# Self-attention's weights turned on VectorE in squares of 32, summed by row tiles of 32 keys, and projected by eight masked products

## What is computed

```python
x = x + self_attention(layernorm(x))        # causal, with a relative-position bias
x = x + cross_attention(layernorm(x), ctx)  # 77 context tokens
x = x + experts(layernorm(x))               # 8 routed experts, top 2, and a shared one
```

```python
q, k, v = split_heads(x @ Wq + bq), split_heads(x @ Wk + bk), split_heads(x @ Wv + bv)
logits = where(j <= i, (q @ k.T + bias(q @ rel_key.T)) * scale, -inf)
attn = softmax(logits)                      # per head, 512 x 512
out = (attn @ v) @ Wo + bo
```

## Time and profile before

| | us |
|---|---|
| median of 3 runs | 501.52 (500.34 to 501.82) |
| profiled execution | 502.75 |
| its span in the profile | 500.9 |
| TensorE busy | 449.2 (90%) |
| VectorE busy | 343.2 (69%) |
| ScalarE busy | 261.3 (52%) |
| GpSimd busy | 162.2 (32%) |

### The profile page before, as it was taken

The page is one execution under the profiler, slowest core; times in us unless marked ns, Lnnn a source line. Parts: engine busy times, 40 slices in busy tenths (PEclk is TensorE's granted clock), DMA queues, the critical chain, the costliest instruction groups (busy, mean ns, idle before and its releaser), DMA issues.

```text
span 500.9 us, 17223 instructions
## 1 busy us (share of the span) xinstructions
PE 449.2 (90%) x7304; PEld 274.7 (55%) x7304; DVE 343.2 (69%) x692; ACT 261.3 (52%) x779; POOL 162.2 (32%) x95
## 2 busy tenths in 40 slices
PE   0758999999999799999799999989887999999997
PEld 0444565665655565655575665565445434666765
DVE  4883788646986847886847887775667587466533
ACT  1133746756556546746534655655443566554653
POOL 7235647322360672351473413075300000001000
PEclk9998999999999889999979999999898999999999
DMA  8111000000000000000000000000000005403150
GB/s 283 56 58 56 13 24 14 12 26 24 24 5 22 21 5 24 25 3 24 7 20 24 3 3 3 3 3 3 1 1 1 2 0 170 166 25 124 67 184 28
DMA packets 17465, 19.49 MB, mean 39 GB/s; under 512 B 1659, under 2 KB 14575, under 8 KB 17263
## 3 DMA queue, kind: packets, MB, share of 16 engines
q1 hardware_dynamic: 17391, 18.41, 11.3%
HBM read 16.17 MB, written 2.16 MB: 37 GB/s over the span
## 4 chain that ended last, share of the span: by engine, by line
PE 67%; DVE 20%; issue 5%; ACT 4%; DMA 2%; POOL 1%; SPq 0%; DVEq 0%; ACTq 0%; POOLq 0%
PE psT L1413 14%; PE psS L1384 13%; PE psS L1394 8%; PE psOM L1353 7%; PE psT L1773 5%; PE psS L1756 4%; DVE neg_max L1039 3%; DVE x_max L1014 2%; PE psS L1603 2%; PE psOM L1494 2%; ACT prob L653 2%; PE psT L1494 2%; PE psOM L1630 1%; DVE prob L1259 1%; DVE stage L878 1%
## 5 line engine op out<-in xcount | busy, mean ns | idle before, releaser
L653 ACT ACTIVATE prob<-psS,neg_max 128x208 f32<-128x208 f32 (+23 forms) x256 | 121.4, 480 | 73.9 <-DVE neg_max L1039 73.8
L1039 DVE TENSOR_REDUCE neg_max<-psS 128x2 f32<-128x672 f32 (+23 forms) x128 | 91.8, 717 | 64.1 <-PE psS L1394 63.2
L444 POOL TENSOR_TENSOR stat<-stat,pack_a_sb 128x4 f32<-128x4 f32 (+2 forms) x16 | 54.7, 3418 | 169.7 <-DVE stat L866 139.3
L1413 PE MATMUL psT<-pack_a_sb,prob 128*128 128x128 f32 (+4 forms) x640 | 99.0, 286 | 6.3 <-DVE pt_even L995 3.3
L1413 PEld LDWEIGHTS psT<-pack_a_sb,prob 128*128 128x128 f32 (+4 forms) x640 | 65.1, 133 | 48.4 <-issue 31.2
L1384 PE MATMUL psS<-k_v,q_both 64*32 64x336 f32 (+23 forms) x2048 | 88.4, 402 | 2.7 <-ACT prob L653 1.5
L1394 PE MATMUL psS<-rel_shifted,q_both 36*32 36x268 f32 (+16 forms) x2048 | 71.5, 337 | 0.0
L478 POOL TENSOR_TENSOR q_both<-qT,pack_a_sb 128x1024 f32<-128x1024 f32 x16 | 31.6, 1973 | 90.7 <-PE psS L1394 82.5
L1394 PEld LDWEIGHTS psS<-rel_shifted,q_both 36*32 36x32 f32 x2048 | 37.2, 109 | 24.7 <-issue 17.6
L653 ACT ACTIVATION_READ_ACCUMULATOR prob<-psS,neg_max 128x1 f32 x256 | 50.6, 197 | 0.0
L1773 PEld LDWEIGHTS psT<-pack_b_sb,prob 128*128 128x128 f32 x288 | 36.1, 191 | 18.6 <-DVE prob L1259 11.4
(11 more groups left out here) (166 smaller groups left out, 597.6 us busy)
## 6 DMA issues: line engine op xcount, KB each, us to landing
q_rep<-q_scratch SPq DMA_DIRECT2D x128, 32.0 KB
k_v<-w_scratch SPq DMA_DIRECT2D x8, 512.0 KB, 6.4
q_both<-w_scratch SPq DMA_DIRECT2D x8, 512.0 KB, 6.3
pack_b_sb<-pack_b_dram SPq DMA_DIRECT2D x1, 1641.5 KB, 10.0
X<-x_dram SPq DMA_DIRECT2D x4, 256.0 KB, 6.0
q_scratch<-qT SPq DMA_DIRECT2D x4, 256.0 KB, 2.0
out_dram<-X SPq DMA_DIRECT2D x4, 256.0 KB, 2.3
pack_a_sb<-pack_a_dram SPq DMA_DIRECT2D x1, 535.0 KB, 4.9
```

What stands on the lines that cost most here:

```text
L444: nc.gpsimd.tensor_tensor(st[:, 5, 0:groups], st[:, 2, 0:groups], ca["root"][0:parts, 0:groups], ALU.pow).then_inc(seeded, 1)
L653: ins = nc.scalar.activation(prob[:, s % 4, half, 0:wide], psS[:, 2 * (s % 2) + half, 0:wide], ACT.Exp, bias=neg_max[:, s % 2, half:half + 1],
L1039: v.tensor_reduce(neg_max[:, s % 2], psS[:, 2 * (s % 2):2 * (s % 2) + 2, 0:wide], AX_X, ALU.max, negate=True).then_inc(max_ready, 1)
L1413: ins = nc.tensor.transpose(psT[0:w, k % 2, at:at + T], prob[:, s % 4, half, j * T:j * T + w], ident)
```

## The change

VectorE turns the weights itself, each 32 x 32 square in place, once a step; the partitions of a square hold four queries of eight heads, so after the turn a row group of 32 partitions holds 32 keys, and its columns are four queries of eight heads. TensorE's transposes, `psT` as their target and all copies out of it go. The weighted sum takes 32 keys at a time as a row tile: all eight heads of a half are the columns of the values (64), the eight heads and 32 queries are the moving columns (256). Each of the four row groups holds other queries and writes a bank of its own (`quarters`: both banks of `psT`, `psO` and `psM`). The result has every head's weights against every head's values, so `finish` scales four quarters (256 elements each) into `sums_of`, and the projection is eight products, one for each head, with `wo_of`, a copy of `wo` in which all but that head's rows are zero. Values go to DRAM and come back with 32 keys on each row group (`store_values`, `load_values`: 4 stores, 16 loads of 256 KB). `prob` has two slots in place of four. Reciprocals are spread at step 0 (was 2), summed at step 1 (was 4), `finish` is at step 5 (was 6), the projection at 6 (was 7), and the sum in three parts at steps 2 to 4 (was four, 2 to 5). Widths are rounded up to 32 keys. Early probes are 14 (was 13), and pieces and probes stand only at steps 6, 7, 0 and 1, as psM is taken at the others. `head_mean` to `head_sum` move two steps or one earlier in a block.

```diff
-        prob = sb("prob", [128, 4, 2, S])
+        prob = sb("prob", [128, 2, 2, S])
+        quarters = [psT[:, 0, 0:HH * 32], psT[:, 1, 0:HH * 32], psO[:, 0:HH * 32], psM[:, 0:HH * 32]]
+        row_sums, projected = psT[:, 1, 256:384], psT[:, 0, 256:384]
...
-            return (blk * BS + (5 if u in (2, 3) else u + 1)) * QG
+            return blk * T + (u // 2 + 1) * 32
+        def turned_to(g, u):
+            blk = ORDER[g % TB]
+            chunks = 4 * (blk + 1)
+            return pt[g % 2][:, 0:2 * chunks * 256].rearrange("p (a c h w) -> p a c w h", a=2, h=HH, w=32) \
+                [:, :, 0:width(blk, u) // 32, 4 * u:4 * u + 4, :]
...
+            def load_values(b):
+                if b > 1:
+                    sp.wait_ge(psO_ready, PRO + (b - 1) * TB)
+                for r in range(4):
+                    sp.dma_start(V_rep[b % 2][32 * r:32 * r + 32],
+                                 v_dram[b].rearrange("(n k) f -> k n f", k=32)).then_inc(v_loaded[b % 2], 16)
...
+                        nc.gpsimd.tensor_tensor(wo_of[:], cb["wo"].unsqueeze(1).to_broadcast([128, HH, D]),
+                                                ca["half_mask"].unsqueeze(2).to_broadcast([128, HH, D]),
+                                                ALU.mult).then_inc(wo_ready, 1)
...
             def finish(k):
                 dve.wait_ge(rec_copied, k + 1)
                 dve.wait_ge(psO_ready, PRO + k + 1)
-                v.tensor_tensor(oT[:], psO[:, 0:T], rec[:], ALU.mult).then_inc(psO_read, 1)
+                if k:
+                    dve.wait_ge(y_ready, k)
+                for r in range(4):
+                    mine = [a.rearrange("p (u q) -> p u q", q=QG)[:, :, QT * r:QT * r + QT] for a in
+                            (rec[:], sums_of[:].rearrange("p h i -> p (h i)"))]
+                    ins = v.tensor_tensor(mine[1].rearrange("p (h u) q -> p h u q", h=HH),
+                                          quarters[r].rearrange("p (h u q) -> p h u q", h=HH, q=QT),
+                                          mine[0].unsqueeze(1).to_broadcast([128, HH, BS, QT]), ALU.mult)
+                ins.then_inc(psO_read, 1)
...
+            def turn(s):
+                g, u = divmod(s, BS)
+                if u == 0 and g >= 2:
+                    dve.wait_ge(psO_ready, PRO + g - 1)
+                dve.wait_ge(scores_read, PRO + s + 1)
+                wide = width(ORDER[g % TB], u)
+                v.transpose(turned_to(g, u),
+                            prob[:, s % 2, :, 0:wide].rearrange("p a (c w h) -> p a c w h", h=HH, w=QT)).then_inc(turned, 1)
...
             for s in range(ALL_STEPS):
-                if g and u == 2:
-                    spread_sums(g - 1)
-                if g and u == BS - 2:
-                    finish(g - 1)
                 dve.wait_ge(scores_ready, s + 1)
                 v.tensor_reduce(neg_max[:, s % 2], psS[:, 2 * (s % 2):2 * (s % 2) + 2, 0:wide],
                                 AX_X, ALU.max, negate=True).then_inc(max_ready, 1)
-                if s >= 2:
-                    copy_units(s - 2)
+                if s:
+                    turn(s - 1)
+                if g and u == 0:
+                    spread_sums(g - 1)
...
-            def project_o(k, w):
-                pe.wait_ge(psO_read, PRO + k + 1)
-                mm(psM[:, T:2 * T], oT[:], w, start=True, stop=True).then_inc(y_ready, 1)
+            def project_o(k):
+                pe.wait_ge(wo_ready, 1)
+                pe.wait_ge(psO_read, PRO + k + 1)
+                pe.wait_ge(y_added, k + ONE)
+                for h in range(HH):
+                    ins = mm(projected, sums_of[:, h, :], wo_of[:, h, :], start=(h == 0), stop=(h == HH - 1))
+                ins.then_inc(y_ready, 1)
...
+            def attend_block(g, part, parts):
...
+                    pe.wait_ge(v_loaded[b % 2], 16 * 4 * (b // 2 + 1))
+                    pe.wait_ge(turned, (g + 1) * BS)
...
+                for c in range(chunks * part // parts, chunks * (part + 1) // parts):
+                    u0 = max(0, 2 * (c - 4 * blk))
+                    for r in range(4):
+                        rows = slice(32 * r, 32 * r + 32)
+                        for half in range(2):
+                            cols = slice(HALF_ROWS * half, HALF_ROWS * (half + 1))
+                            w, to = mine[rows, half, c], quarters[r][cols]
+                            if u0:
+                                w, to = (a.rearrange("p (h w) -> p h w", h=HH)[:, :, 4 * u0:] for a in (w, to))
+                            ins = mm(to, V_rep[b % 2][rows, c, cols], w, start=(c == 0), stop=(c == chunks - 1))
...
             for s in range(ALL_STEPS):
                 g, u = divmod(s, BS)
                 scores(s)
-                if s >= 2:
-                    transpose_weights(s - 2)
-                if g and 2 <= u <= 5:
-                    attend_block(g - 1, u - 2)
+                if g and 2 <= u <= 4:
+                    attend_block(g - 1, u - 2, 3)
```

More of the change, by code:

```diff
@@ L387, in _ @@
                 store_queries(b)
+            for b in range(B):
+                store_values(b)
+            sp.wait_ge(v_stored, 16 * B)
+            load_values(0)
+            load_values(1)
             sp.wait_ge(q_stored, 16 * B)
             load_queries(0, blocks()[2:], True)
-            with sp.Fori(1, B) as b:
+            load_queries(1, blocks(), True)
+            for b in range(2, B):
+                load_values(b)
                 load_queries(b, blocks(), True)
@@ L470, in prepare, with copy_values @@
                                         ALU.add).then_inc(bias_added, 1)
+            def copy_values():
+                pool.wait_ge(ctx_v_copied, 1)
+                pool.wait_ge(psO_ready, PRO + (B - 1) * TB)
+                nc.gpsimd.memset(V_now[0:M], 0.0).then_inc(x_v_ready, 1)
+                pool.wait_ge(x_v_ready, 1)
+                mine = V_now[0:M].rearrange("p t (q r) c -> p t q r c", r=2)
+                for i in range(2):
+                    nc.gpsimd.memset(mine[:, :, :, i, 2 * HD + i:2 * HD + i + 1], 1.0)
+                    ins = nc.gpsimd.tensor_copy(
+                        mine[:, :, :, i, i * HD:i * HD + HD],
+                        ctx_v[:].rearrange("p (t q r d) -> p t q r d", t=B, r=2, d=HD)[:, :, :, i, :])
+                ins.then_inc(x_v_ready, 1)
             def build_queries(b, first):
@@ L530, in _ @@
                 build_queries(b, False)
-            def copy_values(first, end):
-                elements = bass.ds((first - 1) % B, end - first)
-                nc.gpsimd.memset(V_now[0:M, first:end], 0.0).then_inc(x_v_ready, 1)
-                pool.wait_ge(x_v_ready, 3 if first == 0 else 1)
-                mine = V_now[0:M, first:end].rearrange("p t (q r) c -> p t q r c", r=2)
-                for i in range(2):
-                    nc.gpsimd.memset(mine[:, :, :, i, 2 * HD + i:2 * HD + i + 1], 1.0)
-                    ins = nc.gpsimd.tensor_copy(
-                        mine[:, :, :, i, i * HD:i * HD + HD],
-                        ctx_v[:].rearrange("p (t q r d) -> p t q r d", t=B, r=2, d=HD)[:, elements, :, i, :])
-                ins.then_inc(x_v_ready, 1)
             root_heads(B - 2)
-            pool.wait_ge(ctx_v_copied, 1)
-            pool.wait_ge(psO_ready, PRO + BLOCKS - 1)
-            copy_values(1, TB)
             pool.wait_ge(hn_done, B)
@@ L656, in _ @@
                 ins.then_inc(scores_read, 1)
-                if g and u == 5:
+                if g and u == 1:
                     copy_inverses(g - 1)
@@ L1078, in _ @@
                     head_multiply(xc_flat, stat, 128)
+                if g and u == 5:
+                    finish(g - 1)
+                if g == 1 and u == 7:
+                    dve.wait_ge(bias_added, B)
+                if g and u == 7:
+                    add_y(g - 1, tile_of(g - 1))
                 if (g, u) in EARLY_PROBES:
@@ L1397, in scores @@
                 ins.then_inc(scores_ready, 1)
[L1399 to L1424 removed]
+            def attend_block(g, part, parts):
+                b, n = divmod(g, TB)
+                blk = ORDER[n]
+                chunks = 4 * (blk + 1)
+                if part == 0:
+                    pe.wait_ge(v_loaded[b % 2], 16 * 4 * (b // 2 + 1))
+                    pe.wait_ge(turned, (g + 1) * BS)
                     pe.wait_ge(psO_read, PRO + g)
+                    pe.wait_ge(y_added, g + ONE)
+                    pe.wait_ge(rec_copied, g + 1)
+                    pe.wait_ge(piece_read, pieces_until(g + 1, 2))
                     pe.wait_ge(x_probe_read, probes_until(g + 1, 2))
```

251 lines of the change are left out of this document (69 added, 182 removed).

## The result

The changed kernel takes 611.33 us (607.34 to 612.15) against 501.67 for the kernel before, a ratio of 1.218 (1.213 to 1.224). The forecast was 512, within 486 to 548. The direction was right, the size wrong by 99 us. The profiled execution took 607.34 us with a span of 605.6.

What follows compares the result with a forecast made beforehand. TensorE's own work was taken to pace the loop before, and the step-by-step maximum of engine work and round trip after. From 502.75 profiled: +17 - 6 + 5 - 6 = 512.75, stated as 512 us, range 486 to 548.

Steps and rivals of the forecast that it cites:

- TensorE relieved by 40 us: Self-attention loop: transposes and old products go, chunks (69 us) and output products (24 us) come, leaving TensorE about 40 us less.
- Chunks of 0.455 us: Weighted sum on TensorE: a chunk of 32 keys, eight products of 256 columns, costs 0.455 us.
- that rival: Weighted sum: weight loads don't overlap, a chunk costs 0.85 us, 15 us more per element, 570 us in all; chance 0.05.
- Eight products, 1.8 to 2.2 us: Output projection on TensorE: eight 128 x 128 products take 1.8 to 2.2 us where one took 0.4; 24 us in all.
- (a): Fourth blocks: with head_sum at step 6, L911 runs before GpSimd starts and its stall goes; minus 6 us.
- The turn free of GpSimd: VectorE's turn, having a single input, doesn't wait for GpSimd; otherwise each block would lose another 2 us.
- Neither engine's sum alone sets the time: Loop of 300 us: neither TensorE's nor VectorE's (about 246 us) total work fills the old time, so busy time would forecast a gain.
- rival at twice the price: VectorE's turn at twice its element price: 73 us more work, 45 us more in all, 557 us; dear turn's chance 0.14.
- step by step: Loop: per step the largest of TensorE's work, VectorE's work and half a round trip; 72.0 us an element against 67.65, plus 17.
- (b): Spread at step 0 meets GpSimd's L488: fifteen waits of 0.5 to 1.5 us, half hidden; plus 5 us.
- (c): Loop: the two-step buffer smooths some of the steps' unevenness, which taking each step's maximum ignores; minus 6 us.
- smoothing wins: Loop: each block takes only its busier engine's sum, 59.6 us an element, 469 us in all; faster by smoothing had chance 0.33.

Runs made afterwards that it cites:

- the run with GpSimd's wait: Kernel before, with GpSimd's building of an element's first block put behind VectorE's spread: 494.80 us, ratio 0.985.
- dense turn: Changed kernel with the turn writing runs of 32 neighbouring words and its readers' views changed to match: 592.71 us, ratio 1.183.
- short filler: Changed kernel plus transposes nobody reads on TensorE, right behind the scores of steps 0, 1, 5 and 6: 579.71 us, ratio 1.153.
- mended kernel: Changed kernel with dense turn, late projection, GpSimd after the spread, finish at the head of step 5, and short filler: 549.72 us, ratio 1.092.
- late projection: Changed kernel with the projection behind the scores of step 7 instead of step 6, its addition in the next block: 592.03 us, ratio 1.180.
- finish-first kernel: Changed kernel with dense turn, late projection, GpSimd after the spread, and finish at the head of step 5: 558.38 us, ratio 1.111.
- GpSimd after the spread: Changed kernel with GpSimd's L488 of a block begun only after VectorE's spread of the block before: 594.24 us, ratio 1.185.
- finish first alone: Changed kernel with one edit, finish at the head of step 5 ahead of that step's maximum and turn: 584.43 us, ratio 1.165.
- narrow turn: Mended kernel with turns of only 64 elements, the weighted sum reading mostly constants: 533.98 us, ratio 1.064; 523 without the added fill.
- earlier sum: Kernel before with head_sum at step 6 in place of 7: 509.10 us, ratio 1.010.

## Why the prediction was right and wrong

**Right.** *TensorE relieved by 40 us*: 38. *Chunks of 0.455 us*: 0.43 at full clock from start to start (219.90 to 220.33 in the changed kernel's timeline), so the weight loads overlap and that rival fell. *The change of tile form, 0.2 us*, for which no row was given: five chunks with the way back to the scores took 2.34 us (219.63 to 221.97), 0.19 more than five times 0.43. *Eight products, 1.8 to 2.2 us*: 2.02 at full clock. *Finish 1.5*: 1.41 (201.03 to 202.44). *(a)*: L911's successor takes 0.195 everywhere. That its stall costs 6 us was right too, by the run with GpSimd's wait; that the move to step 6 earns them isn't shown, and in the kernel before the same move cost 7. *The turn free of GpSimd*: 1.94 us for 1024 elements in the loop against 1.91 alone. *Neither engine's sum alone sets the time* held as well.

Two stretches of the changed kernel's timeline, chunks of one step and a projection, both at full clock:

```profile
219.90 0.39 PE L1392 MATMUL psT<-pt_even,k_v 32*64 32x256 f32 x4
...
220.33 0.39 PE L1392 MATMUL psT<-pt_even,k_v 32*64 32x256 f32 x4
...
221.97 0.40 PE L1346 MATMUL psS<-k_v,q_both 64*32 64x96 f32 x16
...
225.04 0.48 PE L1346 MATMUL psS<-k_v,q_both 64*32 64x128 f32 x13
...
227.47 2.02 PE L1321 MATMUL psT<-wo_of,sums_of 128*128 128x128 f32 x16 [1.69 <-issue]
229.43 0.45 PE L1346 MATMUL psS<-k_v,q_both 64*32 64x128 f32 x16
```

**The turn was mis-sized.** I took the copy's rate, 92 us in all; it was 142.7, and the rows that spoke for the higher price, GpSimd's scattered words, were nearer. The rival at twice the price gave 45 us for 73 more on VectorE; for 51 more that is 31. The dense turn alone brought 19, with 5 us more of waiting in the spread.

**The step that failed** is the table "step by step". It took the largest of three for each step, all at durations from rows at full clock, and gave 72.0 us for an element; it was 407 / 4 = 101.8. Measured from the first scores of each step to those of the next, in the mean of the four elements:

| block of an element | steps 2 to 4, forecast | measured | the other five, forecast | measured |
|---|---|---|---|---|
| first | 5.3 | 7.1 | 11.4 | 15.7 |
| second | 7.8 | 9.8 | 9.9 | 15.9 |
| third | 7.7 | 8.9 | 13.6 | 19.4 |
| fourth | 8.3 | 10.0 | 8.0 | 15.0 |

Steps 2 to 4 missed by 6.7 us an element, the others by 23.1. The largest part is step 6, from the scores through the wait for finish to the end of the projection: 7.3 us on average, where it took 2.1 in the kernel before. The table was also set against the first element alone (67.65). That one took 90.0 here. The later three have layer norm and pieces that the table doesn't name, and took 100.1, 105.7 and 111.3, where they took 74.8, 79.9 and 77.4.

Two things were missing, the clock and the handovers. *The clock.* The table itself left TensorE partly idle in five of eight steps, and rows 8 showed a clock of 0.50 in such a stretch. I named that as a condition ("I would be too low") and gave it no term, no rival and no chance. The changed kernel spent 142 us of its loop under a clock of 0.75, and the short filler shows at least 32 us of that on the path. The Trainium skill ("TensorE: Matmul & The Clock Gate", section "What's actually happening") says that the clock follows how busy the engine has lately been; the windows above agree.

*The handovers.* The table's third term, half a round trip, knows scores, maximum and exponentials, but not that the projection of step 6 waits for finish, finish for a maximum and a turn, and the scores of step 7 for the projection. I wrote that VectorE idles during the projection, and costed step 6 of the fourth block at 2.1 us; it took 5.8 on average, and 4.39 where the clock stayed full (225.04 to 229.43). In the third block of the timeline above it is 8.64 (197.58 to 206.22). Moving the projection brought 19 us, finish first 27, singly; in one kernel they aren't additive.

**(b) was right in its place and too small**: plus 5, where taking the lock away brought 17. My sign for it failed: 7 of the 16 spreads were held up (0.93 to 2.43 us), not most. **(c), minus 6 for smoothing, isn't borne out.** If buffering recovered anything, more was lost beside it: even the mended kernel needs 344.8 / 4 = 86.2 us an element, and 79.5 with nearly free turns, against 59.6 in the rival "smoothing wins". That rival had 0.33 of my chance and no run came near it. A slip without weight: 16 chunks are 14.5 full ones, not 14.7; the 6.6 us are those of 14.5.

**What the parts sum to.** Dense turn, late projection and GpSimd's wait bring 50 us of the 110 together, finish first 3 (within the noise) and filler 9: 62. Of the 48 that remain, turns account for 27 by one run and, from the finish-first kernel, the eight products for 20 by another. No run combines these two, so whether they make up the rest isn't shown. The loops in windows of 1 us, as above:

| loop of | work at full clock | added by the slow clock | idle |
|---|---|---|---|
| the kernel before | 282 | 6 | 12 |
| the changed kernel | 244 | 60 | 102 |
| GpSimd after the spread | 244 | 48 | 97 |
| late projection | 243 | 53 | 90 |
| dense turn | 244 | 59 | 87 |
| finish first alone | 246 | 46 | 87 |
| short filler alone | 283 | 33 | 66 |
| dense turn, late projection, GpSimd after the spread | 245 | 39 | 71 |
| and finish first | 245 | 42 | 69 |
| and filler | 282 | 15 | 46 |
| and the narrow turn | 281 | 7 | 31 |

Each single edit lowers both idle time and what the slow clock adds, so the 110 us can't be divided between clock and waiting to the microsecond. The last row is telling: with the clock all but full, turns all but free and no lock, TensorE is still idle for 19 us more than before, and the filler fills what the change had saved it.

## What to carry to other kernels

When a change takes work from the engine that sets the pace, ask where in time its pauses come to lie, not only how long they are: behind pauses of 1.6 us (earlier sum) and 3.4 us (changed kernel) TensorE ran at half clock here, so price the work behind such a pause at both levels. Follow each in-order queue past the new instructions and write down who stands behind each wait; a small lock in front of a chain costs more than its own length (here 17 us for 7.7). And look first for stalls in the kernel as it is: one wait on GpSimd gave 1.5% here, where rebuilding the step lost 22%.

## What was unexpected of the hardware

A turn of 32 x 32 squares in fp32 runs at 1.04 ns an element with dense or 8-byte-spaced output, and at 1.69 to 1.79 from 16 bytes on; 16 bytes apart costs as much as 128 (1987 and 1906 ns for 1024 elements). A copy within SBUF runs at 0.52 ns dense, (694 - 293) / 768, and at 0.97 spread by the same layout, (1153 - 411) / 768. Adding 39 us of useless work to TensorE made a kernel 32 us faster. Shorter turns on VectorE made its spread wait longer for GpSimd: 14.5 us in all became 19.6 and 29.8.
